# Two linear attentions in single fp32 products, the second value projection moved ahead of the query transposes, the last bias and the operand sums moved

## What is computed

```python
# first linear attention, 8 heads of 64, inputs xn = layernorm(x)
q_ = relu(q) + scale;  k_ = relu(k) + scale
kv = einsum('bnhe,bnhf->bhef', k_, v);  k_sum = sum(k_, axis=1)
z = 1.0 / (einsum('bnhe,bhe->bnh', q_, k_sum) + EPS)
out = einsum('bnhe,bhef->bnhf', q_, kv) * z[..., None]
out = out.reshape(B, N, C) @ W_proj.T + b_proj
# second linear attention
q = softmax(proj(Wq, bq), axis=-1);  k = softmax(proj(Wk, bk), axis=-1);  v = proj(Wv, bv)
D_inv = 1.0 / (q * k.sum(axis=2, keepdims=True)).sum(axis=-1, keepdims=True)
context = einsum('bhtd,bhte->bhde', k, v)
out = (einsum('bhtd,bhde->bhte', q, context) * D_inv + q) @ Wp.T + bp
# the layers
xn = layernorm(x);  x = x + gnn0(xn, edges) + mix0(xn);  x = x + ffn0(layernorm(x))
xn = layernorm(x);  x = x + gnn1(xn, edges) + mix1(xn);  x = x + ffn1(layernorm(x))
```

## Time and profile before

| | before |
|---|---|
| three runs, us | 2601.41, 2605.64, 2610.76; median 2605.64 |
| profiled execution, us | 2606.16, its span 2604.4, mean granted TensorE clock 0.955 |
| busy in the span, us | PE 2438.6 (94%), PEld 2040.8 (78%), DVE 1810.0 (69%), ACT 935.9 (36%), POOL 1651.5 (63%) |
| chain of waits that ended last | PE 84%, DVE 9%, POOL 2%, issue 2%, ACT 2%, DMA 1% |

### The profile page before, as it was taken

One profiled execution on the slowest core, in us unless ns is written; L12 is line 12 of the kernel. 1 busy time (PEld: TensorE's weight loads), 2 busy tenths in 40 slices (PEclk: granted clock), 3 DMA queues, 4 the chain that ended last, 5 costly groups with the idle time before them and its releaser, 6 DMA issues.

```text
span 2604.4 us, 34428 instructions
## 1 busy us (share of the span) xinstructions
PE 2438.6 (94%) x11600; PEld 2040.8 (78%) x11600; DVE 1810.0 (69%) x2653; ACT 935.9 (36%) x1144; POOL 1651.5 (63%) x722
## 2 busy tenths in 40 slices
PE   6989978886899669999999999999999999999999
PEld 6878867775899567777777877777777777877777
DVE  8974235646698758777777777777777777777775
ACT  3731226622499542222233222332222322223221
POOL 0033313227888846777777777777777777777773
PEclk9998879987799869999999999999999999999999
DMA  3024010021433211122221212212122121221211
GB/s 77 16 77 154 17 65 17 1 71 33 118 91 92 63 38 65 65 97 72 89 97 64 97 71 90 97 64 97 70 91 97 64 97 69 92 97 64 97 65 36
DMA packets 49889, 190.90 MB, mean 73 GB/s; under 512 B 13300, under 2 KB 17911, under 8 KB 33444
## 3 DMA queue, kind: packets, MB, share of 16 engines
q1 hardware_dynamic: 35728, 177.90, 19.6%
q0 software_dynamic: 13200, 10.75, 1.9%
q10 hardware_dynamic: 900, 1.44, 0.2%
HBM read 177.54 MB, written 12.35 MB: 73 GB/s over the span
## 4 chain that ended last, share of the span: by engine, by line
PE 84%; DVE 9%; POOL 2%; issue 2%; ACT 2%; DMA 1%; SPq 0%; DVEq 0%; ACTq 0%; POOLq 0%
PE PS L1718 25%; PE PS L1720 25%; PE PS L1719 25%; PE PS L1982 3%; PE PS L1983 2%; PE PS L1796 2%; POOL gatW L752 1%; DVE hotS L1157 1%; DVE hotD L1158 1%; DVE negmax L1404 1%; DMA fil<-filters 1%; DVE XN L1121 0%; DVE XTl L1130 0%; PE PS L1940 0%; DVE PTl L1418 0%
## 5 line engine op out<-in xcount | busy, mean ns | idle before, releaser
L1668 DVE SCALAR_TENSOR_TENSOR XN<-PS,attn,XN 125x512 f32<-125x512 f32 x1083 | 805.1, 748 | 441.3 <-PE PS L1720 432.8
L787 POOL TENSOR_TENSOR OPl<-TS,OPh 128x1024 fp32r<-128x1024 f32 x256 | 676.6, 2643 | 117.8 <-ACT OPh L1067 117.8
L787 POOL TENSOR_TENSOR OPl<-RAW,OPh 128x1024 fp32r<-128x1024 f32 x192 | 554.6, 2889 | 274.7 <-ACT OPh L1067 274.6
L1718 PE MATMUL PS<-OPh,XTh 128*125 128x512 f32 x1280 | 507.1, 396 | 2.0 <-DVE attn L1622 2.0
L1720 PE MATMUL PS<-OPh,XTl 128*125 128x512 f32 x1280 | 505.7, 395 | 0.0
L1719 PE MATMUL PS<-OPl,XTh 128*125 128x512 f32 x1280 | 503.4, 393 | 0.0
L1067 ACT ACTIVATE OPh<-TS 128x1024 fp32r<-128x1024 f32 x256 | 271.7, 1062 | 529.1 <-PE PS L1720 519.2
L1067 ACT ACTIVATE OPh<-RAW 128x1024 fp32r<-128x1024 f32 x192 | 204.1, 1063 | 580.9 <-PE PS L1720 580.9
L1718 PE MATMUL PS<-OPh,Sh 128*125 128x512 f32 x1024 | 404.8, 395 | 4.2 <-DVE XN L1665 4.2
L1720 PE MATMUL PS<-OPh,Sl 128*125 128x512 f32 x1024 | 403.9, 394 | 0.0
L1719 PE MATMUL PS<-OPl,Sh 128*125 128x512 f32 x1024 | 402.6, 393 | 0.0
(11 more groups left out here) (350 smaller groups left out, 3560.7 us busy)
## 6 DMA issues: line engine op xcount, KB each, us to landing
RAW<-in_values SPq DMA_DIRECT2D x64, 2048.0 KB, 7.5
filters<-filt SPq DMA_DIRECT2D x14, 672.0 KB
fil<-filters SPq DMA_DIRECT2D x11, 840.0 KB
Wraw<-in_ffn SPq DMA_DIRECT2D x4, 1024.0 KB, 5.7
Wraw<-in_L_q SPq DMA_DIRECT2D x2, 1024.0 KB, 5.1
Wraw<-in_L_k SPq DMA_DIRECT2D x2, 1024.0 KB, 8.2
Wraw<-in_L_v SPq DMA_DIRECT2D x2, 1024.0 KB, 7.1
gatW<-nodes,dstI POOLq DMA_INDIRECT x90, 3.7
```

What stands on the lines that cost most here:

```text
L787: g.tensor_tensor(OPl[:, j], operand_source(j, parity), OPh[:, j].bitcast(F32), ALU.subtract).then_inc(op_lower, 1)
L1668: v.scalar_tensor_tensor(out=XN[:, t], in0=PS[0:P, bank, :], scalar=w, in1=XN[:, t], op0=ALU.mult, op1=ALU.add).then_inc(v_added, 1)
L1718: mm(dst, lh, rh, start=start, stop=False, skip_group_check=resumed)
```

## The change

1. Both linear attentions keep queries, keys, values and the key-value matrix as single fp32 buffers; their products are one `mm` each instead of a `product` of three. ACT's roundings and DVE's subtractions of these operands go, and with them `full` and `value_ready`. The blocks of kv are copied by ACT (`first_blocks`, partitions 0 to 63) and by DVE (`second_blocks`, 64 to 127), whose last small copy waits for ACT. The transposed queries of the second attention are copied by ACT alone.
2. `v2` stands ahead of `qT2` in UNITS and in PE's program; DVE writes the low part of v2's weight one step earlier in its softmax loop.
3. The bias of proj2 is added by DVE, behind its last `msgl`, instead of by POOL. POOL's four sums wait for `msg_lower` of the last round, and no longer for DVE's steps of the last chunk but one.

The core of the diff:

```diff
-UNITS += [(s, i) for s, n in (("xt2", T), ("hn", 2), ("q2", 3), ("k2", 3), ("qT2", T), ("v2", 3), ("kv2", 1)) for i in range(n)]
+UNITS += [(s, i) for s, n in (("xt2", T), ("hn", 2), ("q2", 3), ("k2", 3), ("v2", 3), ("qT2", T), ("kv2", 1)) for i in range(n)]
...
-BY_SCALAR = {"score", "ov1"}
-
-SPLIT = {"xt0", "xwl", "q0", "k0", "v0", "kv0", "ct0", "xt1", "q1", "k1", "v1", "probT", "attn",
-         "xt2", "k2", "v2", "qT2", "kv2", "ct2", "xt3", "outT"}
...
+SPLIT = {"xt0", "xwl", "kv0", "ct0", "xt1", "q1", "k1", "v1", "probT", "attn", "xt2", "kv2", "ct2", "xt3", "outT"}
...
@@ -757,12 +746,7 @@
             pool.wait_ge(filled, NUMBER[("xt2", T - 1)] + 1)
             for t in range(ET):
                 gather(t)
-            pool.wait_ge(rows2_loaded, 2 * LANDED)
-            wait_drained(pool, ("proj2", 2))
-            g.tensor_tensor(X[:], X[:], rows[:, 1:2, :].to_broadcast([P, T, D]), ALU.add).then_inc(x_bias2, 1)
-
-
-            pool.wait_ge(edge_step, EDGE_STEPS * NB * (NCH - 1))
+            pool.wait_ge(msg_lower, NB * NCH)
             pool.wait_ge(v_loaded[0], 16)
             raw = RAW[:, 0]
             g.tensor_tensor(TS[:, 0], raw[:, 1, 0:2], raw[:, 0, 0:2], ALU.subtract).then_inc(t_summed, 1)
...
-            def blocks_upper(stage, kvh, zeroed):
+            def first_blocks(stage, kv, zeroed):
 
                 u = ("kv" + stage, 0)
                 wait_filled(u)
-                act.wait_ge(zeroed, 2)
-                for h, o in enumerate((0, DH)):
-                    parts = pair_blocks(slot(u)[o:o + DH])
-                    a.activation(in_banks(kvh[o:o + DH, :, o:o + DH]), parts[:, :, :, o:o + DH], ACT.Copy)
-                    last = a.activation(in_banks(kvh[o:o + DH, :, 2 * DH + h:2 * DH + h + 1]), parts[:, :, :, 2 * DH:2 * DH + 1], ACT.Copy)
-                last.then_inc(upper_ready, 1)
+                act.wait_ge(zeroed, 1)
+                parts = pair_blocks(slot(u)[0:DH])
+                a.activation(in_banks(kv[0:DH, :, 0:DH]), parts[:, :, :, 0:DH], ACT.Copy)
+                upper(u, in_banks(kv[0:DH, :, 2 * DH:2 * DH + 1]), parts[:, :, :, 2 * DH:2 * DH + 1])
...
-            for n in range(7):
+            for n in range(6):
 
                 if n == 3:
                     weight_upper(WEIGHT["L1_v"])
-                if n < 6:
-                    exponentials("q2" if n < 3 else "k2", n % 3, n, TILES[n % 3])
-                if n >= 4:
-                    m = n - 4
-                    u, tiles = ("k2", m), TILES[m]
-                    act.wait_ge(value_ready, n_full[0] + m + 1)
-                    upper(u, K2h[:, tiles[0]:tiles[-1] + 1], full2[0:P, m % 3, 0:len(tiles) * D].rearrange("p (t d) -> p t d", d=D))
+                exponentials("q2" if n < 3 else "k2", n % 3, n, TILES[n % 3])
             weight_upper(WEIGHT["L1_p"])
             for j in range(T):
                 u = ("qT2", j)
                 wait_filled(u)
-                upper(u, Q2h[:, :, tile_columns(j)], slot(u)[:, 0, 0:K * P].rearrange("p (k n) -> p k n", k=K))
...
-            blocks_upper("2", KV2h, bd2_zeroed)
...
+                a.activation(Q2[:, :, tile_columns(j)], slot(u)[:, 0, 0:K * P].rearrange("p (k n) -> p k n", k=K), ACT.Copy).then_inc(drained_s, 1)
+            first_blocks("2", KV2, bd2_zeroed)
...
+            def shifted_relu(unit, dst, rows_, cols, width):
+
                 wait_filled(unit)
...
+                v.tensor_scalar(dst, slot(unit)[0:rows_, 0:cols, 0:width], 0.0, DH ** -0.5, ALU.max, ALU.add).then_inc(drained_v, 1)
...
-                rest(u, VAl[:, j, :, 0:2 * DH], by_pair(slot(u)[0:P, 0:len(tiles), :]), VAh[:, j, :, 0:2 * DH])
-            def blocks_rest(stage, kvh, kvl, zeroed):
-                for b in (kvh, kvl):
-                    v.memset(b[:].bitcast(F32), 0.0).then_inc(zeroed, 1)
+                    wait_filled(("agg", 2))
+                    v.memset(VA[:, :, :, 2 * DH:VW], 1.0).then_inc(v_padded, 1)
+                wait_filled(u)
+                v.tensor_copy(VA[:, j, :, 0:2 * DH], by_pair(slot(u)[0:P, 0:len(tiles), :])).then_inc(drained_v, 1)
...
+            def second_blocks(stage, kv, zeroed):
+
+                v.memset(kv[:], 0.0).then_inc(zeroed, 1)
                 u = ("kv" + stage, 0)
+                wait_filled(u)
+                dve.wait_ge(zeroed, 1)
+                parts = pair_blocks(slot(u)[DH:2 * DH])
+                v.tensor_copy(in_banks(kv[DH:2 * DH, :, DH:2 * DH]), parts[:, :, :, DH:2 * DH])
                 dve.wait_ge(upper_ready, splits(u))
-                dve.wait_ge(zeroed, 2)
-                for h, o in enumerate((0, DH)):
-                    parts, c = pair_blocks(slot(u)[o:o + DH]), slice(o, o + DH)
-                    sums = slice(2 * DH + h, 2 * DH + h + 1)
-                    v.tensor_tensor(in_banks(kvl[c, :, c]), parts[:, :, :, c], in_banks(kvh[c, :, c]).bitcast(F32), ALU.subtract)
-                    ins = v.tensor_tensor(in_banks(kvl[c, :, sums]), parts[:, :, :, 2 * DH:2 * DH + 1],
-                                          in_banks(kvh[c, :, sums]).bitcast(F32), ALU.subtract)
-                ins.then_inc(drained_v, 1)
-
-            blocks_rest("0", KVh, KVl, bd_zeroed)
+                v.tensor_copy(in_banks(kv[DH:2 * DH, :, 2 * DH + 1:VW]), parts[:, :, :, 2 * DH:2 * DH + 1]).then_inc(drained_v, 1)
+
+            second_blocks("0", KV, bd_zeroed)
...
-            for n in range(8):
-                if n == 5:
+            for n in range(7):
+                if n == 4:
...
+            v.memset(V2[:, :, :, 2 * DH:VW], 1.0).then_inc(v_padded, 1)
...
-                buf = buffer2_for(u)
                 wait_filled(u)
-                z = buf[0:P, 0:nt * D].rearrange("p (t d) -> p t d", d=D)
-                v.tensor_tensor(z, slot(u)[0:P, 0:nt, :], rows[:, 0:1, :].to_broadcast([P, nt, D]), ALU.add).then_inc(value_ready, 1)
-                rest(u, V2l[:, j, :, 0:2 * DH], by_pair(z), V2h[:, j, :, 0:2 * DH])
+                v.tensor_tensor(V2[:, j, :, 0:2 * DH], by_pair(slot(u)[0:P, 0:nt, :]),
+                                by_pair(rows[:, 0:1, :].to_broadcast([P, nt, D])), ALU.add).then_inc(drained_v, 1)
             split_weight(WEIGHT["L1_p"])
-            blocks_rest("2", KV2h, KV2l, bd2_zeroed)
+            second_blocks("2", KV2, bd2_zeroed)
...
             lower(NB * NCH - 1, 0)
+            wait_drained(dve, ("proj2", 2))
+            v.tensor_tensor(X[:], X[:], rows[:, 1:2, :].to_broadcast([P, T, D]), ALU.add).then_inc(x_bias2, 1)
             dve.wait_ge(scattered, NB * NCH)
...
-                        ins = product(slot(u)[:, r // 2, i:i + VW], (kh[:, t, c], kl[:, t, c]), (vh[:, t, r], vl[:, t, r]), t == 0, t == T - 1)
+                        ins = mm(slot(u)[:, r // 2, i:i + VW], keys[:, t, c], values[:, t, r], start=t == 0, stop=t == T - 1)
...
-                            ins = product(slot(u)[0:P, r // 2, i:i + VW], (qh[:, r, c], ql[:, r, c]), (bh[:, r], bl[:, r]), True, True)
+                            ins = mm(slot(u)[0:P, r // 2, i:i + VW], queries[:, r, c], kv[:, r], start=True, stop=True)
...
             node_rows("q2", WEIGHT["L1_q"])
             node_rows("k2", WEIGHT["L1_k"])
+            node_rows("v2", WEIGHT["L1_v"])
             wait_drained(pe, ("q2", 2))
             transposes("qT2", None, QS)
-            node_rows("v2", WEIGHT["L1_v"])
-            linear_attention("2", K2h, K2l, V2h, V2l, Q2h, Q2l, (KV2h, KV2l), QS)
+            linear_attention("2", K2, V2, Q2, KV2, QS)
```

More of the change, by code:

```diff
@@ L280, in build @@
                 XWl = sb("XWl", [P, T, D], F32R, s)
-                sb("above_XW", [P, 2 * T * PAIRS * (VW - 2 * DH)], F32, s)
-                QTh = sb("QTh", [128, K, NT], F32R, s)
-                QTl = sb("QTl", [128, K, NT], F32R, s)
+                QT = sb("QT", [128, K, NT], F32, s)
                 sig = sb("sig", [P, T, D], F32, s)
-                full = sb("full", [128, 3, 1024], F32, s)
-                KVh = sb("KVh", [128, PAIRS, VW], F32R, s)
-                KVl = sb("KVl", [128, PAIRS, VW], F32R, s)
+                KV = sb("KV", [128, PAIRS, VW], F32, s)
         with ExitStack() as s:
-            KEh = sb("KEh", [P, T, D], F32R, s)
-            KEl = sb("KEl", [P, T, D], F32R, s)
+            KE = sb("KE", [P, T, D], F32, s)
         with ExitStack() as s:
@@ L917, in _ @@
                 act.wait_ge(f_stored[i], LANDED * FPAIRS)
-            for f in range(K):
-                upper_of_full(("q0", f), QTh[:, f], lambda b: b[:, 0:NT])
-                if f == 0:
-                    act.wait_ge(f_scaled, HALVES)
-                    weight_upper(2)
+            act.wait_ge(f_scaled, HALVES)
+            weight_upper(2)
             weight_upper(3)
@@ L928, in _ @@
             weight_upper(4)
-            for m, tiles in enumerate(TILES):
-                upper_of_full(("k0", m), KEh[:, tiles[0]:tiles[-1] + 1],
-                              lambda b: b[0:P, 0:len(tiles) * D].rearrange("p (t d) -> p t d", d=D))
             weight_upper(5)
```

(29 more changed lines are left out.)

88 lines of the change are left out of this document (15 added, 73 removed).

## The result

Medians of four runs each: 2559.5 us (2554.7 to 2563.7) against 2607.3 us (2601.4 to 2610.8): ratio 0.9821, 95% interval 0.9805 to 0.9837, 46.7 us by the ratio and 47.8 by the medians. The forecast was 2569, its range 2558 to 2584: the way is right, the gain is 9.5 us larger than forecast. The profiled executions give 2604.4 and 2556.1 us of span, 48.3 less; PE is busy for 37.9 us less (2400.7), DVE for 30.4 (1779.6), the mean clock is 0.971 instead of 0.955.

A forecast was written before the change was run, and what follows sets the result against it. The prediction took PE at the lower clock to bound the first attention and POOL's gather stream the edge stage. 2606.2 - 14.1 (first attention) - 9.2 (second) - 1.0 (stream) - 12.6 (stage end) = 2569.3, so 2569 us; range 2558 to 2584.

The forecast's parts named there:

- Price of a plain product: First attention: a plain fp32 product is 2 records, 0.43 us at the lower clock, against 0.64 for three split instructions.
- Rival A: Attention products: plain ones cost four steps where the split has three, so kv0 and num0 lengthen; 2590 us, chance 0.04.
- D: First attention: a plain product is paid by instruction, not by column, so the kernel gets slower; 2630 us, chance 0.02.
- kv0 at the upper level: First attention: kv0's plain products run at the upper clock, 4.4 us instead of 12.4, saving 8.0 us.
- the copies' 1.2: Behind kv0: ACT copies the upper half beside DVE's lower half, about 0.9 us instead of 2.13, saving 1.2.
- num0: First attention: num0 has 20 records fewer at 0.21 us, saving 4.2 us; up to 8.2 at the upper clock.
- Second attention, 9.2: Value projection moves ahead of query transposes, so gathers start 9.2 us earlier; kv2 starting about 20 us earlier is otherwise hidden.
- Gather stream, 1.0: Edge stage: gathers take 1 us less with some DVE work gone, between 4 less and 5 more.
- Rival C: Gather stream gives its 9.2 us back, as more gathers lie beside dense DVE work and big loads; 2579, chance 0.13.
- End of the stage, 12.6: Edge stage end, without POOL's bias and sums: last round starts 8.3 us earlier, two products save 4.3, together 12.6.
- at best 2 us more: PE's last two edge rounds, partly at the lower clock, were left as they are; at best 2 us more gain.
- Rest: From 985 us on, value products keep PE full to the end; nothing changes there and they shift as a block.

The follow-up runs named there:

- kv0_split: The kernel after, with each kv0 product issued three times in reduced precision on single operands; kv0's 60 records took 6.89 us at clock 1.00.
- rounds_late: The kernel after, with DVE waiting before its first edge round until the 55th gather has landed; 2562.0 us.
- end_alone: The kernel before, with only the bias moved to DVE and POOL's sums put behind DVE's last remainder; 2591.2 us, ratio 0.9956.
- fp32_alone: The kernel after, with value projection order and end of the edge stage as before, so single fp32 products alone; 2581.4 us, ratio 0.992.
- end_undone: The kernel after, with bias and operand sums on POOL directly behind the last gather, as before; 2574.5 us.
- sums_early: The kernel after, with POOL's four sums directly behind the last gather again, the bias staying on DVE; 2569.1 us.
- num0_split: The kernel after, with each num0 product issued three times in reduced precision on single operands, kv0 plain; num0 to proj0 8.40 us.
- clock_b: The kernel after, with second-attention products issued three times in reduced precision and the plain first attention's pauses drawn out by DVE copies to 1.71 and 2.08 us.

## Why the prediction was right, and where it was short

- **Price of a plain product**: right. 2 records of 0.12 us at 1.00 (4.70 us for 40), where kv0_split gives 0.115 for a split record (6.89 for 60). Rivals A and D, dearer plain products, are refuted.
- **kv0 at the upper level**: right, 7.7 us for the forecast 8.0, and 1.3 for the copies' 1.2. The reason given for the old clock, that the split products bring it down, is only half of it (kv0_split): they did not within kv0, but they keep it down.
- **num0**: mis-sized by a choice of the wrong clock level. "PE pauses between tiles, which before went with 0.50. I take 4.2": the pauses came, of 0.49, 0.37 and 0.17 us, and the clock stayed at 1.00; it saved 7.8, within the bound of 8.2. It is 3.6 of the 11.4 us by which the saving in the traces (48.3) differs from the forecast (36.9).
- **Second attention, 9.2**: right, 9.3, and that no more of the 20 us counted is borne out by rounds_late. Its origin was told too simply: the wait goes in two parts, 5.6 by the products and 3.7 by the order.
- **Gather stream, 1.0**: this is the term that was sized worst. It gave 6.9 in the two traces, beyond the bound of 4, and is 5.9 of the 11.4. Two things are in it. Before had three slow gathers in this stretch (4.65, 4.65 and 4.37 us) and after two (4.65 each): 2.8 us, luck. The rest is 4.1: with slow gathers counted as average ones the stretch takes 244.0 us in both profiles with the stream of before (before, end_alone) and 238.5 to 242.2 in the nine with that of after. So the ordinary gathers did become faster, by 0.03 us each, four times what was forecast. That the removed DVE work does it, as the prediction had it, is not shown. Rival C, that the stream gives 9 us back, is refuted.
- **End of the stage, 12.6**: 14.9. Of this 8.8 come by the start of the last round (3.3 instead of 12.1 us behind the last gather; forecast 8.3), 4.3 by its products, exactly as forecast, and 1.8 by PE's last rounds (9.73 instead of 11.55 us behind the last `msgl`). These were the "at best 2 us more" that the prediction named and counted as nothing: they ran partly at 0.50 before, and at 1.00 after. That PE's stand behind the held DVE brings this is likely, not shown: from the last `msgl` to `aggT` it is 11.6 to 12.5 us in the four kernels with the sums early (before, fp32_alone, end_undone, sums_early) and 8.9 to 9.7 in nine of the ten others, but 11.2 in num0_split, where nothing was held. The bias on DVE cost nothing; POOL's sum waited for it instead.
- **Rest**: `aggT` to the end is the same within 0.1 us in the two profiles, so the last part moved as a block.

The result stands at the lower edge of the range because three terms missed the same way: num0, which was taken at its cautious end, and the stream and the end of the stage, which were not and came out above their upper bounds (6.9 over 4, 14.9 over 14.6). The saving of 48.3 us between the two profiles lies beyond the 46 that the prediction had as its most. The two us added for the spread of the runs kept the median inside; that part is luck.

## What to carry to other kernels

Where products are narrow, look at the time of a record and not at the count of passes: a split product of 130 columns pays three times what a plain one pays twice. What POOL does on large tensors right behind its last transfer holds DVE just when DVE should take that transfer's data: let it wait for DVE's last step instead. Where DVE was held for long, PE stood with it and came back at the lower clock, for 1.8 to 2.7 us more. And in a stage paced by a stream of transfers, what starts earlier beside it is worth nothing; only the stream's own waits and its first and last element count.

## What the runs showed of the hardware

- Price and width of a plain product, by the groups of after (count | busy us, mean ns):

```profile
L1612 PE MATMUL PS<-OPh,XTh 128*125 128x512 f32 x1280 | 507.3, 396 | 2.0 <-DVE attn L1516 2.0
L1680 PE MATMUL PS<-radial,W1d 60*96 60x500 f32 x28 | 13.4, 598 | 0.0
```

Plain products of 314 columns (`out_s`) and of one column (`ones`, a window at clock 0.50), in after:

```profile
877.41 0.42 PE L1884 MATMUL PS<-aggT,out_s 64*128 64x314 f32 x1
877.67 0.43 PE L1884 MATMUL PS<-aggT,out_s 64*128 64x314 f32 x1
332.00:336.00 4.00, 4.00 (x20) 4.00 (x20) 0.00 (x0) 0.00 (x0) 0.00 (x0) 0.50 0.00 0
```

At clock 1.00, from start to start, a split record takes 0.11 us at 130 columns, 0.145 at 314 (`hotE,msgh`) and 0.23 at 512 (584.70, 584.93). A plain record takes 0.11 at 130, 0.26 at 314 and 0.42 at 500, and comes twice. So a plain product costs 0.22, 0.53 and 0.84, and a split one 0.34, 0.44 and 0.69: the gain here is one of narrow products and turns into a loss at wide ones, already at 314, if those of `out_s`, on 64 rows with the same of `out_v` beside them, may stand for full ones. Narrower is no cheaper for the plain form: at clock 0.50 a record takes some 0.2 us with one column (20 in 4 us), and 0.213 with 128. The Trainium skill (FP8 and Floating Point Precision, TensorE Precision Notes) has four passes for true fp32. The trace agrees at all three widths: the split record of 512 columns gives 0.23 / 512 us a column, and four times that is 0.23 at 130, 0.56 at 314 and 0.90 at 500, where 0.22, 0.53 and 0.84 were measured. What does not follow the width is the split record: at 130 columns it takes 0.11 and not 0.06. Rival A of the prediction went wrong there, in the price of the split product and not in the count of passes.

- DVE and POOL hold each other by whole instructions, both ways: DVE's 1 us of one-hot writes took 11.49 behind POOL's bias and first sums, POOL's sum 4.90 instead of 2.4 beside DVE's add. A gather of POOL (31st to last, in after, the two slow ones left out) takes 1.21 us on average when no DVE instruction overlaps it, 1.67 when `msgl` does and 1.40 beside others of DVE.
- The clock can stay at 0.50 for 16 us while PE is busy without a pause, if it runs narrow split products; plain ones, as busy, had it back at 1.00 after some 3 us (kv0_split, clock_b; one profile each).
